# Attention scores from two float32r parts in 64-row tiles, two heads at a time

## The reference, cut to what matters

```
Q = norm(x) @ Wq + bq;  K = ctx @ Wk + bk;  V = ctx @ Wv + bv       # per head 16 deep
A = softmax(Q K^T / 4)      # phases 0 and 6; phase 4: sigmoid, no bias
x = x + (A V) @ Wo + bo
```

## Time and profile before

| | |
|---|---|
| three runs | 3310.57, 3314.86, 3318.32 us, median 3314.86 |
| the profiled execution | 3315.56 us; its span 3313.7 us, first to last instruction |
| TensorE (PE) busy | 2999.2 us, 91% of the span |
| VectorE (DVE) busy | 1761.3 us, 53% |
| ScalarE (ACT) busy | 1611.1 us, 49% |
| GpSimd (POOL) busy | 382.8 us, 12% |
| phases 0, 4, 6 | about 57 to 880, 1600 to 2165, 2400 to 3220 us |

### The profile page before, as it was taken

How to read it: one execution, slowest core, us unless ns; L and a number is a source line. 1 busy time by engine, 2 the same in 40 slices (tenths; PEclk the granted TensorE clock), 3 DMA queues, 4 the chain that set the end, 5 groups by cost and what they waited for, 6 DMA issues and landing times.

```text
span 3313.7 us, 42625 instructions
## 1 busy us (share of the span) xinstructions
PE 2999.2 (91%) x16108; PEld 1521.6 (46%) x16108; DVE 1761.3 (53%) x4116; ACT 1611.1 (49%) x2747; POOL 382.8 (12%) x357
## 2 busy tenths in 40 slices
PE   5899999999799889997899999979889999999987
PEld 2234343343377658887332333257533433434333
DVE  3877776778275553332211110046477777777834
ACT  1465665656500112111577777922226656566662
POOL 3000100000110102223100010022301010000000
PEclk7999999999899999998999999989889999999996
DMA  6323224221110001000834432120243233232100
GB/s 159 83 59 77 62 51 89 54 47 24 48 34 26 1 13 45 1 1 20 198 77 105 100 86 61 24 78 1 58 104 64 66 76 62 66 76 47 24 1 30
DMA packets 119187, 190.36 MB, mean 57 GB/s; under 512 B 15900, under 2 KB 82628, under 8 KB 115912
## 3 DMA queue, kind: packets, MB, share of 16 engines
q1 hardware_dynamic: 118984, 187.65, 24.4%
HBM read 133.59 MB, written 53.63 MB: 56 GB/s over the span
## 4 chain that ended last, share of the span: by engine, by line
PE 74%; DVE 11%; ACT 6%; issue 6%; DMA 2%; SPq 1%; POOL 1%; POOLq 0%; ACTq 0%; DVEq 0%
PE psum L189 58%; PE psum L613 15%; DVE mpart L761 4%; ACT probs L665 3%; DVE rest L734 1%; ACT kp L715 1%; PE psum L274 1%; DMA qst<-q_parts_dram 1%; DVE rest L732 1%; DVE vt L752 1%; SPq L886 0%; DVE stats L301 0%; DVE x L1196 0%; ACT kp L709 0%; DMA kst<-k_parts_dram 0%
## 5 line engine op out<-in xcount | busy, mean ns | idle before, releaser
L665 ACT ACTIVATE probs<-psum 128x512 f32<-128x512 f32 (+3 forms) x2080 | 1270.8, 685 | 461.3 <-PE psum L189 459.0
L761 DVE TENSOR_REDUCE mpart<-psum 128x1 f32<-128x400 f32 (+1 forms) x2048 | 1033.4, 566 | 163.3 <-PE psum L189 161.9
L189 PE MATMUL psum<-qst,kst 115*128 115x512 bf16 (+3 forms) x2496 | 848.0, 383 | 29.3 <-ACT probs L665 20.4
L189 PE MATMUL psum<-kst,qst 112*128 112x400 bf16 (+1 forms) x2048 | 692.3, 343 | 60.7 <-DMA qst<-q_parts_dram 28.9
L613 PE MATMUL psum<-probs,vt 128*17 128x512 f32 (+1 forms) x4992 | 657.2, 598 | 33.0 <-ACT probs L665 32.7
L189 PEld LDWEIGHTS psum<-kst,qst 112*128 112x128 bf16 x2048 | 202.0, 99 | 585.2 <-DVE mpart L761 306.6
L189 PEld LDWEIGHTS psum<-qst,kst 115*128 115x128 bf16 (+3 forms) x2496 | 231.4, 100 | 428.6 <-issue 183.5
L613 PEld LDWEIGHTS psum<-probs,vt 128*17 128x17 f32 (+1 forms) x4992 | 83.1, 95 | 260.7 <-issue 167.5
L189 PE MATMUL psum<-ctxT,wk 128*128 128x512 f32 (+1 forms) x384 | 152.7, 528 | 24.5 <-DMA ctxT<-in_ctxT 21.7
L189 PE MATMUL psum<-wv,ctxT 128*128 128x256 f32 (+1 forms) x624 | 160.6, 404 | 8.5 <-ACT hT L288 4.8
L189 PE MATMUL psum<-masked_hi,w_hi 128*128 128x256 f32 x512 | 153.4, 300 | 7.9 <-DVE masked_lo L1803 7.9
(11 more groups left out here) (273 smaller groups left out, 3246.3 us busy)
## 6 DMA issues: line engine op xcount, KB each, us to landing
kst<-k_parts_dram SPq DMA_DIRECT2D x96, 600.4 KB, 8.9
k_parts_dram<-kp SPq DMA_DIRECT2D x24, 1200.8 KB, 4.4
q_parts_dram<-qp SPq DMA_DIRECT2D x168, 128.0 KB
qst<-q_parts_dram SPq DMA_DIRECT2D x48, 448.0 KB, 11.2
ctxT<-in_ctxT SPq DMA_DIRECT2D x36, 512.0 KB, 4.9
kst<-k_parts_dram SPq DMA_DIRECT2D x48, 200.1 KB, 10.4
stage<-in_L_ffn_W SPq DMA_DIRECT2D x16, 256.0 KB, 4.1
x<-in_x SPq DMA_DIRECT2D x4, 512.0 KB, 8.4
```

The lines of the kernel that those rows point to most:

```text
L189: last = e.matmul(dst, lhsT, rhs, start=i == 0, stop=i == len(pairs) - 1)
L665: e.activation(self.probs[n % slots][0:kn, :, :], c.psum[0:kn, k:k + self.wide, :], ACT.Exp if softmax else ACT.Sigmoid, scale=DH ** -0.5) ...
L761: e.tensor_reduce(self.mpart[:, row, i:i + 1], c.bank(k)[:, 0:MAX_BLOCKS[i][1]], AX.X, ALU.max).then_inc(c.drained(k), 1)
```

## The change

Keys and queries are cut into two parts in float32r (rounded float32 that TensorE takes in one pass) in the place of three in bfloat16. Per head three products of parts (hi hi, lo hi, hi lo) stand on 3 x 16 = 48 partitions, with two rows for the maximum 50. Two heads lie in one tile, the first from partition 0, the second from partition 64, and their matmuls are issued one after the other into neighbouring banks. A group of four heads is now made of two heads from each half of the 16 (the weights' columns `wo` and `bv` are laid out for it), so `k_hi`, `k_lo`, `q_hi`, `q_lo` hold everything of a batch.

- For a key or query block ScalarE copies PSUM to a float32 tile (phase 4: VectorE), and GpSimd makes both parts from it: a copy to float32r, and a subtraction. VectorE has no part in it under softmax. The values' copy out of PSUM goes from VectorE to ScalarE in phases 0 and 6. Their bias is folded into the output's once per phase (step "fold").
- The stores to DRAM and the reads are gone. A unit is loaded by twelve DMAs from SBUF to SBUF, each of 16 partitions.
- The step "unit" of unit u is placed at u - 1.98 (for the first unit of a batch u - 1.43) in the place of u - 1.98 for all; all keys of the next batch lie from 1.15 to 2.3 of a batch's first unit, its queries to 2.5, in the place of 0.28 to 2.5. Before the first key block of a batch the engine that copies it waits until the last three units of the batch before are loaded.
- Maxima are made by groups of two banks (4 and 5) and one (6), by turns, each 402 keys wide, reduced by one instruction per group: 21 pairs and 22 singles per unit. Exponentials go by groups of two banks (0 and 1) and one (2): 17 pairs and 18 singles. Phase 4 keeps its 26 pairs. The probabilities have 12 slots in the place of 10.
- The maximum's rows: one transpose in float32, a copy (ScalarE) and a subtraction (VectorE), four small DMAs. They are placed to end at u - 0.23.
- The normalised rows of x have two buffers in the place of four, so the second pair of rows waits for the first pair's transpose.

```diff
-MAX_SPLIT = 4
-MAX_BLOCKS = [(CTX * i // MAX_SPLIT, CTX * (i + 1) // MAX_SPLIT - CTX * i // MAX_SPLIT) for i in range(MAX_SPLIT)]
-K_PART = [0, 1, 2, 0, 1, 2, 0]
-Q_PART = [0, 0, 0, 1, 1, 1, 2]
-PAIR_ROWS = DH * len(K_PART)
-MAX_ROWS = 3
-STACK = PAIR_ROWS + MAX_ROWS
-LEAD = 0.182
+MAX_SPLIT, MAX_WIDTH = 4, 402
+MAX_STARTS = [0, 400, 800, CTX - MAX_WIDTH]
+PAIRS = GROUP // 2
+PART_ROWS = 3 * DH
+STACK = PART_ROWS + 2
+MAX_GROUPS = [group for i in range(0, 63, 3) for group in (([i, i + 1], 4), ([i + 2], 6))] + [([63], 4)]
...
-                ("n_rows", f, b, 0), ("n_rows", f, b, 2), ("idle",), ("n_turn", f, b, 0), ("n_turn", f, b, 2)]
+                ("n_rows", f, b, 0), ("idle",), ("n_turn", f, b, 0), ("n_rows", f, b, 2), ("idle",), ("n_turn", f, b, 2)]
...
-            if n > 2:
-                k, v = c.at(c.nth_step["n_turn", n - 2])
+            if n > 1:
+                k, v = c.at(c.nth_step["n_turn", n - 1])
...
-        self.kp = [c.sbuf(sc, "kp", [P, 3, CTX], BF16) for _ in range(KC)]
-        self.qp = [c.sbuf(sc, "qp", [P, 3, SEQ], BF16) for _ in range(KC)]
-        self.rest = [c.sbuf(sc, "rest", [P, BANK]) for _ in range(2)]
+        self.k_hi, self.k_lo = c.sbuf(sc, "k_hi", [P, PAIRS, CTX], F32R), c.sbuf(sc, "k_lo", [P, PAIRS, CTX])
+        self.q_hi, self.q_lo = c.sbuf(sc, "q_hi", [P, PAIRS, SEQ], F32R), c.sbuf(sc, "q_lo", [P, PAIRS, SEQ])
         self.vt = [c.sbuf(sc, "vt", [P, len(KEY_CHUNKS), HEADS, VW]) for _ in range(2)]
...
+        self.kst = [c.sbuf(sc, "kst", [P, PAIRS, CTX], F32R) for _ in range(3)]
+        self.qst = [c.sbuf(sc, "qst", [P, PAIRS, SEQ], F32R) for _ in range(3)]
+        self.probs = c.sbuf(sc, "probs", [P, PROBS, BANK])
...
+            self.score_groups = [group for i in range(0, count - GROUP, 3) for group in (([i, i + 1], 0), ([i + 2], 2))]
+            self.score_groups += [([count - 4, count - 3], 0), ([count - 2], 2), ([count - 1], 0)]
+        else:
+            self.score_groups = [([i, i + 1], i % 6) for i in range(0, count, 2)]
...
-        put(self.key_steps(0, 0), -3.5, -2.5, prelude)
...
+        put(self.key_steps(0), -3.5, -2.3, prelude)
...
+        put(self.query_steps(0), -2.3, -2.1, prelude)
+        for u in range(3):
+            put([("unit", f, u)], -2.05 + 0.3 * u, -2.05 + 0.3 * u)
...
+                put(self.key_steps(b + 1), first + 1.15, first + 2.3, misc)
+                put(self.query_steps(b + 1), first + 2.3, first + 2.5, misc)
...
+            if u >= 3:
+                at = u - 1.98 + (0.55 if u % GROUPS == 0 else 0)
+                put([("unit", f, u)], at, at)
...
-                if h == qt == i == 0:
+                _, _, u, s = step
+                if s == 0:
                     self.wait_unit(e, u)
-                mm(e, bank[:, 0:kn], [(self.qst[u % 3][0:PAIR_ROWS, h, qt * P:(qt + 1) * P],
-                                       self.kst[u % 3][0:PAIR_ROWS, h, k0:k0 + kn])]).then_inc(c.filled(k), 1)
+                for n, block in enumerate(MAX_GROUPS[s][0]):
+                    j, i, qt, p = block % 2, block // 2 % MAX_SPLIT, block // 8 % 4, block // 32
+                    k0, at = MAX_STARTS[i], slice(64 * j, 64 * j + PART_ROWS)
+                    t = mm(e, c.bank(k + n)[:, 0:MAX_WIDTH], [(self.qst[u % 3][at, p, qt * P:(qt + 1) * P],
+                                                               self.kst[u % 3][at, p, k0:k0 + MAX_WIDTH])])
+                t.then_inc(c.filled(k), 1)
...
+                for n, block in enumerate(self.score_groups[s][0]):
+                    kc, h = divmod(block, GROUP)
+                    (k0, kn), p, at = KEY_CHUNKS[kc], h // 2, slice(64 * (h % 2), 64 * (h % 2) + rows)
+                    t = mm(e, c.bank(k + n)[0:kn, :], [(self.kst[u % 3][at, p, k0:k0 + kn], self.qst[u % 3][at, p, :])])
...
+            if kind in ("keys", "query") and softmax:
+                (k, v), (raw, _, bias) = c.at(step), self.split_of(step)
+                self.wait_parts_loaded(e, step)
+                e.wait_ge(c.filled(k), v)
+                if step[2:] == (0, 0, 0):
+                    self.wait_key_weights(e)
+                elif step[2:] == (0, 0):
+                    self.wait_weights(e)
+                e.activation(raw, c.bank(k)[:, 0:raw.shape[1]], ACT.Identity, bias=bias).then_inc(c.drained(k), 1)
+            elif kind == "values" and softmax:
+                k, v = c.at(step)
+                src, dst = self.values_of(step)
+                self.wait_values(e, step)
+                e.wait_ge(c.filled(k), v)
...
+                blocks, slot = self.score_groups[s][0], self.exp_slot[step]
+                kn = KEY_CHUNKS[blocks[-1] // GROUP][1]
+                if self.exp_after[step]:
+                    e.wait_ge(*self.pv_done(*self.exp_after[step]))
+                e.wait_ge(c.filled(k), v)
+                e.activation(self.probs[0:kn, slot:slot + len(blocks), :], c.psum[0:kn, k:k + len(blocks), :],
                              ACT.Exp if softmax else ACT.Sigmoid, scale=DH ** -0.5).then_inc(c.drained(k), 1)
...
+    def wait_parts_loaded(self, e, step):
+        b = step[2]
+        if b and step[3:] in ((0,), (0, 0)):
+            for u in range(GROUPS * b - 3, GROUPS * b):
+                self.wait_unit(e, u)
...
+                e.tensor_reduce(self.mpart[:, blocks[0]:blocks[0] + m], c.psum[:, k:k + m, 0:MAX_WIDTH], AX.X,
                                 ALU.max).then_inc(c.drained(k), 1)
...
+                (k, v), (raw, hi, _) = c.at(step), self.split_of(step)
+                e.wait_ge(c.drained(k), v)
+                a = c.pool.count(e.tensor_copy(hi, raw))
+                e.wait_ge(c.pool.sem, a)
+                e.tensor_tensor(raw.bitcast(F32R), raw, hi.bitcast(F32), ALU.subtract).then_inc(c.sem("split_made"), 1)
...
+                here, there = c.sem(f"unit_in{u % 3}"), self.split_n["query", f, b, PAIRS - 1]
+                e.wait_ge(c.sem("split_made"), max(there, self.split_n["keys", f, b, PAIRS - 1, len(KEY_BLOCKS) - 1]))
+                if softmax and u < 3:
...
+                for j in range(2):
+                    src = slice(32 * g + DH * j, 32 * g + DH * j + DH)
+                    for i in range(3):
+                        dst = slice(64 * j + DH * i, 64 * j + DH * i + DH)
+                        k_part = self.k_lo[src, :, :] if i == 1 else self.k_hi[src, :, :].bitcast(F32)
+                        q_part = self.q_lo[src, :, :] if i == 2 else self.q_hi[src, :, :].bitcast(F32)
+                        e.dma_start(self.kst[u % 3][dst, :, :].bitcast(F32), k_part).then_inc(here, 16)
+                        e.dma_start(self.qst[u % 3][dst, :, :].bitcast(F32), q_part).then_inc(here, 16)
...
+                for j in range(2):
+                    for i, part in enumerate((self.m_hi, self.m_lo)):
+                        row = 64 * j + PART_ROWS + i
+                        dst = self.qst[u % 3][row:row + 1, :, :].bitcast(F32).rearrange("p h (a q) -> p (h a) q", q=P)
...
```

More of the change, by code:

```diff
@@ L134, in number @@
         self.nth_step[step[0], self.count[step[0]]] = step
-        for j in range(banks if ring else 0):
-            k = ring.next()
+        for j in range(0 if ring is None else banks):
+            k = ring if type(ring) is int else ring.next()
             self.visits[k] += 1
@@ L270, in tensor @@
             for j in range(2):
[L271 removed]
+                h = c.hrow[j]
                 for q in range(KC):
@@ L529, in tensor @@
         c, f, softmax, norm = self.c, self.f, self.softmax, self.norm
-        rows = STACK if softmax else PAIR_ROWS
+        rows = STACK if softmax else PART_ROWS
         for step in self.order:
             kind = step[0]
-            if kind in ("keys", "query", "values", "proj", "den", "div", "max", "max_turn"):
+            if kind in ("keys", "query", "values", "proj", "den", "div", "max", "max_turn", "scores", "fold"):
                 k, v = c.at(step)
@@ new lines, in vector @@
+            if kind in ("keys", "query") and not softmax:
+                (k, v), (raw, _, _) = c.at(step), self.split_of(step)
+                self.wait_parts_loaded(e, step)
+                e.wait_ge(c.filled(k), v)
+                e.tensor_copy(raw, c.bank(k)[:, 0:raw.shape[1]]).then_inc(c.drained(k), 1)
+            elif kind == "values" and not softmax:
+                k, v = c.at(step)
+                src, dst = self.values_of(step)
+                self.wait_values(e, step)
+                e.wait_ge(c.filled(k), v)
+                e.tensor_copy(dst, src).then_inc(c.drained(k), 1)
+            elif kind == "fold":
+                k, v = c.at(step)
+                self.wait_weights(e)
+                e.wait_ge(c.filled(k), v)
+                e.tensor_tensor(self.bo[:, :], self.bo[:, :], c.bank(k)[:, 0:DM], ALU.add).then_inc(c.drained(k), 1)
```

367 lines of the change are left out of this document (135 added, 232 removed).

## The result

The kernel after takes 3618.8 us in the median of four runs (3600.18 to 3626.28), beside 3313.83 for the kernel before: a ratio of 1.091, 95% interval 1.0864 to 1.0958. The prediction was 3064, 2945 to 3225, with 0.13 for slower. It went the other way by 305 us. Each time is the start of one evacuation of a unit to that of another (line 672 before, 716 after; in phase 4 789 and 809).

The account below looks back on a forecast made before the run. TensorE was taken as the bound, except at phase 4's end (ScalarE). From the profiled 3315.6 us, gains of 309 less costs of 50 (loads) and 8 (row buffers) gave 3064.6, taken as 3064, range 2945 to 3225.

Parts of the forecast that it names:

- The main term: TensorE, softmax units: two heads' matmuls on partition halves run at once, 14.4 us for 22.3, a gain of 7.9 a unit.
- a slot of 1.3 times the price: TensorE's paired matmuls: if two row tiles lost as four do, softmax gain 3.6 us a unit, end near 3180.
- The slower rival: TensorE: the two halves don't run at once, 23.6 us for 22.3 a unit; 3410 us, chance 0.14.
- point of decision: TensorE's softmax matmuls: with 70 slots, costs of 58 us are met when a slot takes 0.29 us, not 0.205.
- The three banks: PSUM banks in softmax units: pairs refilled only after VectorE reads both, a unit keeps 47 us; 3197 us, chance 0.21.
- The loads: Unit loads at a batch's start: 12 us from issue to landing, 8.4 us lost at three batches in two phases, 50 us.
- Its second term: A batch's first key copy: ScalarE waits 3.4 us for a load issued 0.2 unit earlier.
- port rule: Loads from SBUF: 16 neighbouring partitions reach four of 16 ports; load 15 us, the cost grows by 18 to 36.
- Phase 4: Score pairs at 0.230 us save 5.4 us a unit; 12 units give 65 us, the last four nothing.
- Small terms: Stores, key splits, row buffers, the maximum's rows and probability slots: near nothing, but 8 us (0 to 20) for the buffers.
- The first maxima of phase 0: Start of a softmax phase, VectorE busy 38.9 of 47.0: pairs and the values' departure take off 5 us, 10 in all.
- the norm's rows: Two buffers of normalised rows: second pair's rows wait behind the first pair's transpose, 8 us (0 to 20).

Follow-up runs that it names:

- single maxima: Kernel after with its maxima one bank at a time, 64 reductions a softmax unit for 43: 3543.58 us, 1.068 of the kernel before.
- filled tiles: Kernel after with one-bank maxima, its softmax maxima and scores reading 62 and 64 rows per half, added rows zero: 3465.04 us, 1.046 of before.
- no loads: Loads after each attention's third unit left out: from the kernel after 3535.67 us; with one-bank maxima and zero-filled rows too, 3408.18 us.
- single exponentials: Softmax exponentials one bank at a time, on the kernel after with one-bank maxima, zero-filled rows and later loads left out: 3355.38 us; unfilled with loads 3578.51.
- the kernel whose runs spread over 52 us: Kernel after with one-bank maxima, zero-filled rows and no loads after each attention's third unit: 3408.18 us, 1.023 of before; 3402.91 without the last run.
- the filled variant: Kernel after with maxima and exponentials one bank at a time, zero-filled rows, no loads after each attention's third unit: 3355.38 us, 1.013 of before.
- the grouped old kernel: Kernel before with maxima and softmax exponentials grouped by two banks and one, maxima 402 wide, 12 probability slots: 3493.0 us, 1.054 of before.

## Why the prediction was wrong

The steps from the kernel after back towards before, by medians: single maxima -75, filled tiles -79, no loads -57, single exponentials -53, which leaves 42 of the 305 us. The sizes depend on the order: the loads give 83 first, and single exponentials cost 35 where tiles are unfilled and loads are there. The third and the fourth hang on the kernel whose runs spread over 52 us; by its other median they are 62 and 48.

**The main term failed, first by its slot.** It was 70 slots of 0.205 us, 14.4 us a unit for 22.3. The number of slots was near (78.0 measured in four units of the batch, the upper end). The slot was not: some 0.107 us stands behind many pairs, and the median of the 258 slots at full clock in the batch after is 0.289 us, of the 346 in the filled variant 0.288. By this median 78 slots are 22.5 us a unit, an estimate, where 22.3 had been: the gain is gone by the slot alone. (The streams and the 0.107 us behind pairs make 19.1 of it, 0.245 a slot; the rest are short waits and changes to another tile shape.) The filled variant at clock 1.00 bears it out with its waits: 25.9 us a unit (103.7/4), 26.4 before. Put into the prediction's sum, 22.5 us in the softmax units and 26 slots of 0.338 in phase 4 give 3338 us in the place of 3064, which is half of the 555 us by which the forecast was off; what is left is the clock, the banks and the loads. I took a pair to be as long as its stream, from the column strips of the earlier trace rows. The trace before held a warning that I passed by: of the 0.98 us that the values' eight matmuls take there, 0.52 lie between the start of the last and the next start of another shape, more than a stream. The prediction had also set a slot of 1.3 times the price beside its sum, 0.27 us, and put the end near 3180 by it; that was nearer to the slot than its own 0.205. The slower rival had the right sign by another mechanism: the halves don't take turns. Its point of decision, 0.29 us, is near the measured slot partly by luck, since it took 70 slots and left out phase 4's gain; with 78 slots and that gain the same working gives 0.28.

**Second, by the clock, for which the sum had no term.** The kernel before is granted full speed over nearly the whole of phase 0, and I took that as given:

```profile
122.90:890.90 768.00, 725.84 (x4093) 286.52 (x4092) 546.30 (x1170) 475.73 (x917) 51.48 (x54) 1.00 0.25 54
```

The same length of the kernel after, from 122 to 890, stands at 0.86. The batch after spends 68 of its 239 us at the lower level. If TensorE held the batch all that time, 34 us of it would be lost, about the whole difference to 203.9; this is an upper bound, since while it is slow it is not always the one waited for. By experiment, zeros in the unused rows give back 79 us, and some 75 without loads; fewer rows in the old kernel take 28 us (80 rows), and 366 and 419 (48 rows).

The Trainium skill (TensorE: Matmul & The Clock Gate, "Terms") says that the chip watches how busy TensorE is and gates its clock by that, and the same page of the Trainium skill ("A second HAM failure mode: psum-queue depth-cycling") names short idles between groups, while cycling through PSUM banks, as a cause. The traces agree in part: clock and waits go together in the kernel after. But the grouped old kernel has those idles at 0.98, and the 48-row one is 99% busy at 0.50. By that rule alone neither would come out so.

**The three banks** were a rival at 0.21, priced at 47 us a unit against 43.1; the forecast itself had put them at nothing. The cost is shown: 179 us on the old kernel, of which 119 by the maxima. Both numbers of busy time that spoke against it were right (VectorE 34.5 a unit for 33.3 forecast, ScalarE 30.3 for 29.3), and did not matter: what counts, as the waits of TensorE for VectorE and ScalarE in that run say, is that it can't refill either bank of a pair until both are read, so a turn of three banks becomes two turns. The pair reduction takes 0.993 us for 0.92 forecast, the single 0.569 for 0.506: busy time divided by the count had been taken for the price of one.

**The loads** were right in kind, one wait of 5.14 us for a load at this batch's start (5 forecast), and under-sized in all: 17 us for 12, since an issue takes up to 2.0 us and not 0.446. Its second term, 3.4 us in which ScalarE waits for a load at a batch's first key, did not come: that line of ScalarE's waits for TensorE alone in the trace (103.1 us in 60 waits, none for a load). 57 to 83 us in the whole for 50, so that total was met partly by luck. The Trainium skill's port rule (SBUF — State Buffer, "Door 1: The DMA port swizzle") gave an estimate of 15 us, with the two heads one after the other; 17.3 us passed from the first issue to the first use. The rows here put 13.1 of them on the issues, and no run tells the ports apart from them.

**Phase 4** was forecast to gain 65 us and gained 10. Four units missed their 127 us by 15.3: the slot is some 8.5 of it (3.2 us a unit saved for 5.4), the load at a batch's start 4.0 (without loads 138.3 us, at a clock of 0.96), and some 3 are left for the clock, which was not tried by itself. Zeros moved the whole by nothing there.

**Small terms.** The first maxima of phase 0 were to gain 5 us; the first evacuation came 11.9 us later. Between phases 4 and 6 21 us were lost, where 8 in the whole had been allowed for the norm's rows.

**Open.** What the last 42 us are was not tried one by one; in that variant the first evacuation is 4 us late and that of phase 6 11, the softmax units take 19 and 25 us more a phase (half of phase 0's in its last three units, 125.3 for 115.4), and phase 4 takes 26 less. What the 0.107 us behind a pair are was not isolated. A change of tile shape costs something without any pair: in the kernel with 48 rows a key projection starts 0.306 us after a score at full clock, for 0.219 before. Nor was it shown whether a `kst` issue is long by its sixteen rows or by its source in SBUF.

## What to carry to other kernels

Read the granted clock of the stretch before any sum, and ask what the change does to it: on this kernel, narrower tiles at the same instruction count lost more by the clock (366 and 419 us with 48 rows for 112) than any queue or wait did, and rows of zeros gave part of it back in the softmax phases, for three memsets each. Price a pair of row tiles by a run or a timeline of such pairs, not by its stream. Grouping two of three PSUM banks into one instruction may save overhead on an engine that has slack; here it made the one that has none wait, 179 us on the kernel before.

## What was not expected of the hardware

- The granted clock fell with the rows that matmuls address, at equal instructions and with TensorE 99% busy: 1.00 with 112 and 115 rows, 0.99 with 80 (204.8 us for the batch, 203.9 before), 0.92 down to 0.72 over four units of phase 0 with 48, 0.50 for a whole unit that has no keys or values of a next batch beside it. Rows of zeros counted as rows.
- A pair of float32r matmuls on 48 to 50 of 64 rows starts together (mostly 3 or 4 ns apart), and what follows starts 0.289 us (402 columns) or 0.337 us (512) after it in the median: 1.2 and 1.3 times the rate of single bfloat16 matmuls at 0.173 and 0.216, not twice.
- A DMA of 16 partitions x 12.8 KB from SBUF to SBUF held SyncE's queue for 1.3 to 2.0 us in five of six issues of a load; the DRAM read before held it for 0.446.
